# A relational graph-convolution kernel: the bias matmuls as a pair over two rows each, interleaved bn_stats, and work moved between the engines

## What is computed

```python
h = jnp.maximum(_layernorm(x, axis=-1), 0.0)          # eps 1e-5, no scale, no shift
x = x + relu( direction(h, W_fwd, Wg_fwd, b_fwd, bg_fwd, adj,   rels 2..40)
            + direction(h, W_bwd, Wg_bwd, b_bwd, bg_bwd, adj_t, rels 2..40)
            + direction(h, W_loop, Wg_loop, b_loop, bg_loop, adj_t, rel 1) )
# direction: hW = h @ W.T;  g = hW @ Wg.T
#   vals_r = (hW + b_r) * sigmoid(g + bg_r)
#   out[n] = sum over r and m of (adj[n, m] == r) * vals_r[m]
```

## Time and profile before

| | |
|---|---|
| runs | 123.61, 123.80, 123.98 us |
| median | 123.8 us |
| span of the profiled execution | 121.9 us (no separate time of this execution is shown) |
| busy in the span: PE, PE weight loads, DVE, ACT, POOL | 107.6, 102.9, 100.7, 103.8, 50.8 us |
| bytes moved | 25.41 MB, mean 208 GB/s |
| busy share of the DMA engines | nearly full until about 73 us, then under half |

### The profile page before, as it was taken

How to read it: one execution, slowest core, us unless ns; L and a number is a source line. 1 busy time by engine, 2 the same in 40 slices (tenths; PEclk the granted TensorE clock), 3 DMA queues, 4 the chain that set the end, 5 groups by cost and what they waited for, 6 DMA issues and landing times.

```text
span 121.9 us, 3211 instructions
## 1 busy us (share of the span) xinstructions
PE 107.6 (88%) x838; PEld 102.9 (84%) x838; DVE 100.7 (83%) x355; ACT 103.8 (85%) x230; POOL 50.8 (42%) x77
## 2 busy tenths in 40 slices
PE   0223999999999999999999999999999999999950
PEld 0012799999999999999999999999999999999940
DVE  3597878998998989898989898989899976666560
ACT  4039959999999999999999999999999999997400
POOL 6185344453627180908172635454363627220000
PEclk9999999999999999999999999999999999999996
DMA  2999999999999999999999980503132231405073
GB/s 57 312 291 255 296 290 292 291 290 295 288 297 280 320 282 278 314 338 323 321 341 317 327 235 16 152 21 114 58 93 79 64 110 33 139 7 170 19 229 104
DMA packets 50313, 25.41 MB, mean 208 GB/s; under 512 B 892, under 2 KB 50304, under 8 KB 50304
## 3 DMA queue, kind: packets, MB, share of 16 engines
q1 hardware_dynamic: 49952, 25.17, 75.4%
q10 hardware_dynamic: 288, 0.13, 0.4%
q0 software_dynamic: 64, 0.00, 0.0%
HBM read 16.91 MB, written 8.39 MB: 208 GB/s over the span
## 4 chain that ended last, share of the span: by engine, by line
PE 85%; DMA 4%; ACT 3%; DVE 2%; issue 1%; POOL 1%; POOLq 0%
PE psum L821 23%; PE psum L797 13%; PE psum L802 13%; PE psum L803 13%; PE psum L804 13%; PE psum L785 11%; DMA bias_in<-in_L_gnn_bg_loop 4%; ACT xn L433 2%; DVE x_all L609 1%; POOL bias_in L355 1%; PE psum L773 1%; DVE hT_lo L594 1%; ACT hT_hi L445 0%; ACT bias_hi L488 0%; ACT w_gT L492 0%
## 5 line engine op out<-in xcount | busy, mean ns | idle before, releaser
L433 ACT ACTIVATE xn<-x_all,shift,rstd 128x128 f32 (+1 forms) x128 | 55.4, 486 | 0.0
L371 POOL TENSOR_TENSOR rstd<-var_eps,minus_half 128x8 f32<-128x8 f32 (+1 forms) x17 | 26.6, 1563 | 50.2 <-DVE var_eps L569 50.2
L802 PE MATMUL psum<-w_hi,hT_hi 128*128 128x256 f32 x128 | 36.5, 285 | 0.0
L803 PE MATMUL psum<-w_lo,hT_hi 128*128 128x256 f32 x128 | 36.4, 284 | 0.0
L804 PE MATMUL psum<-w_hi,hT_lo 128*128 128x256 f32 x128 | 36.3, 283 | 0.0
L821 PE MATMUL psum<-vals,mask 128*128 128x128 f32 x256 | 33.5, 274 | 0.0
L584 DVE TENSOR_TENSOR vals<-psum,gate 128x512 f32<-128x512 f32 (+1 forms) x33 | 22.3, 675 | 11.3 <-ACT gate L457 11.3
L821 PEld LDWEIGHTS psum<-vals,mask 128*128 128x128 f32 x256 | 31.1, 191 | 0.0
L538 DVE BATCH_NORM_STATS2 stats<-x_all 128x6 f32 (+1 forms) x128 | 27.5, 278 | 2.3 <-DMA x_all<-in_x 2.1
L797 PE MATMUL psum<-bias_rows,ones_r 128*128 128x512 f32 x64 | 28.5, 445 | 0.2 <-DVE hT_lo L594 0.2
L803 PEld LDWEIGHTS psum<-w_lo,hT_hi 128*128 128x128 f32 x128 | 24.6, 192 | 2.9
(11 more groups left out here) (41 smaller groups left out, 36.7 us busy)
## 6 DMA issues: line engine op xcount, KB each, us to landing
adj_all<-in_adj SPq DMA_DIRECT2D x16, 512.0 KB, 6.6
x_all<-in_x SPq DMA_DIRECT2D x15, 512.0 KB, 5.8
out<-x_all SPq DMA_DIRECT2D x15, 512.0 KB, 3.3
x_all<-in_x SPq DMA_DIRECT2D x2, 256.0 KB, 3.7
out<-x_all SPq DMA_DIRECT2D x2, 256.0 KB, 2.4
w_raw<-in_L_gnn_W_loop ACTq DMA_DIRECT2D x1, 64.0 KB, 3.0
w_raw<-in_L_gnn_Wg_loop ACTq DMA_DIRECT2D x1, 64.0 KB, 3.8
bias_in<-in_L_gnn_b_loop POOLq DMA_DIRECT2D x1, 1.0 KB, 4.3
```

The costliest lines, as they stand in the source:

```text
L371: pool.tensor_tensor(rstd[:, p, cols], var_eps[:, p, cols], minus_half[:, cols], ALU.pow).then_inc(ready, 1)
L433: last = nc.scalar.activation(xn[:, s, j * D:j * D + D], x_all[:, bass.ds(g * GC + j * D, D)], ACT.Identity, bias=shift[:, p, k:k + 1], sc ...
L802: nc.tensor.matmul(to, hi, w_hi[:, :], start=False, stop=False)
L803: nc.tensor.matmul(to, hi, w_lo[:, :], start=False, stop=False)
```

## The change

The bias matmuls contract over two rows each. `ones_r`, `bias_in`, `bias_hi` and `bias_rows` have 64 partitions; the bias vectors are broadcast to all 64 by two loads from ACT's queue, issued after those of the weights. Rows 0 and 1 serve the first two graphs, rows 32 and 33 the other two, which lie in another group of 32 rows of the array. Both matmuls now stand ahead of all twelve products. The remainder is computed on all 64 partitions, and then four one-row copies put the high part on rows 0 and 32. `past` and `zeros` are gone.

bn_stats reads two graphs alternately, so that what it gives for the even elements is one graph's mean and variance and for the odd elements the other's. The seven small DVE instructions are gone, and POOL makes mean and variance with two instructions of its own ahead of the power. DVE normalises the fourth graph of each group, ACT the other three. The order of a step changes on ACT (relu, normalise, gate of t + 1, watch) and on DVE (messages, output, low_part, normalise, row_stats), without a special order for the start. POOL's steps are written out without a loop, coefficients ahead of the mask.

```diff
-            pool.dma_start(bias_in[:, 0, :], b_loop.to_broadcast([2, D])).then_inc(bias_loaded, 16)
-            pool.dma_start(bias_in[:, 1, :], bg_loop.to_broadcast([2, D])).then_inc(bias_loaded, 16)
...
+            def coefficients(p, lo, hi, var_done, at, done):
+
+                st = stats[:, p, lo // 2:hi // 2, :].rearrange("p k (e f) -> p k e f", e=2)
+                pool.tensor_scalar(var_eps[:, p, lo:hi].rearrange("p (k e) -> p k e", e=2), st[:, :, :, 2],
+                                   1.0 / D, EPS, ALU.mult, ALU.add).then_inc(var_done, 1)
+                pool.tensor_scalar(mean_neg[:, p, lo:hi].rearrange("p (k e) -> p k e", e=2), st[:, :, :, 1],
+                                   -1.0, 0.0, ALU.mult, ALU.add).then_inc(var_done, 1)
+                pool.wait_ge(var_done, 3 * at - 1)
+                pool.tensor_tensor(rstd[:, p, lo:hi], var_eps[:, p, lo:hi], minus_half[:, lo:hi], ALU.pow
+                                   ).then_inc(var_done, 1)
...
+            for t in range(-NORM, GROUPS):
+                if t == -NORM or (t % CHUNK == 0 and live(t + COEF)):
+                    c = (t + COEF) // CHUNK
+                    pool.wait_ge(stats_ready, c + 1)
+                    if c >= 2:
+                        pool.wait_ge(normed_dve, c * CHUNK - CHUNK)
+                        pool.wait_ge(normed_act, c * CHUNK - CHUNK)
+                    coefficients(c % 2, GROUP if c == 0 else 0, CG, var_ready, c + 1, coef_ready)
                 if live(t + MASK):
-                    edges(t + MASK, chunk_after(c, phase, MASK), (phase + MASK) % UNROLL)
...
+                    edges(t + MASK)
...
             def step(t, c, phase):
...
-                if live(t):
-                    sigmoid(t, phase)
-
-                if live(t + NORM):
-                    normalise(*norm, range(0, GROUP // 2))
                 if live(t + HT):
                     relu_turned(t + HT, (phase + HT) % UNROLL)
                 if live(t + NORM):
-                    normalise(*norm, range(GROUP // 2, GROUP))
+                    normalise(t + NORM, chunk_after(c, phase, NORM), (phase + NORM) % UNROLL)
+                if live(t + PROD):
+                    sigmoid(t + PROD, (phase + PROD) % UNROLL)
                 if (phase + 1) % CHUNK == 0 and live(t + 1):
                     watch(chunk_after(c, phase, 1), (phase + 1) % UNROLL)
 
+            act.dma_start(bias_in[:, 0:D], b_loop.to_broadcast([64, D])).then_inc(bias_loaded, 16)
+            act.dma_start(bias_in[:, D:2 * D], bg_loop.to_broadcast([64, D])).then_inc(bias_loaded, 16)
...
-                for j in range(GROUP):
+                if phase % CHUNK == 0 and late(g, 2 * CHUNK):
+                    dve.wait_ge(coef_ready, c - 1)
+                for j in range(0, GROUP, 2):
+                    k = (phase % CHUNK * GROUP + j) // 2
+                    last = nc.vector.bn_stats(
+                        stats[:, p, k, :],
+                        x_all[:, bass.ds(g * GC + j * D, 2 * D)].rearrange("p (b d) -> p d b", b=2))
...
+                for j in range(ON_ACT, GROUP):
                     k = phase % CHUNK * GROUP + j
...
+                    last = nc.vector.tensor_scalar(
+                        xn[:, s, j * D:j * D + D], x_all[:, bass.ds(g * GC + j * D, D)],
+                        mean_neg[:, p, k:k + 1], rstd[:, p, k:k + 1], ALU.add, ALU.mult)
+                last.then_inc(normed_dve, 1)
...
                 dve.wait_ge(bias_hi_ready, 1)
+                for n in range(2):
+                    nc.vector.tensor_tensor(bias_rows[:, n, :], bias_in[:, :], bias_hi[:, :].bitcast(FP32),
+                                            ALU.subtract).then_inc(bias_step, 1)
                 dve.wait_ge(bias_step, 2)
-                for n in range(2):
...
+                for at in (0, 32):
+                    for n in range(2):
+                        nc.vector.tensor_copy(bias_rows[at:at + 1, n, :], bias_hi[at:at + 1, :].bitcast(FP32)
+                                              ).then_inc(bias_step, 1)
...
+                if is_number(t, -3):
+                    split_weights()
+                    split_bias()
                 if live(t):
                     messages(t, phase)
-                if chunk_done:
-                    sums(*of)
                 if live(t - 1):
                     output(t - 1, (phase - 1) % UNROLL)
...
                 if live(t + HT):
                     low_part(t + HT, (phase + HT) % UNROLL)
...
+                if live(t + NORM):
+                    normalise(t + NORM, chunk_after(c, phase, NORM), (phase + NORM) % UNROLL)
+                if live(t + STATS):
+                    row_stats(t + STATS, chunk_after(c, phase, STATS), (phase + STATS) % UNROLL)
...
-                pe.wait_ge(normed, g + 1)
+                pe.wait_ge(normed_act, g + 1)
+                pe.wait_ge(normed_dve, g + 1)
...
-                for q in range(0, GROUP, 2):
-                    nc.tensor.matmul(prod_ps[s][:, q:q + 2, :, :], ones_r[:, :], bias_rows[:, :, :],
-                                     start=True, stop=False)
-                    for j in (q, q + 1):
-                        hi, lo = (h[:, s, j * N:j * N + N] for h in (hT_hi, hT_lo))
...
+                for n in range(2):
+                    nc.tensor.matmul(prod_ps[s][:, 2 * n:2 * n + 2, :, :], ones_r[32 * n:32 * n + 2, :],
+                                     bias_rows[32 * n:32 * n + 2, :, :], start=True, stop=False)
+                for j in range(GROUP):
+                    hi, lo = (h[:, s, j * N:j * N + N] for h in (hT_hi, hT_lo))
...
```

More of the change, by code:

```diff
@@ L245, in steps @@
                 step(t, t // CHUNK, t % UNROLL)
-        def filling(t):
-            return isinstance(t, int) and t < FILL_TO
         def is_number(g, n):
@@ L389, in edges @@
+            def edges(g):
+                if g % CHUNK == 0:
+                    arrived(pool, adj_loaded, g // CHUNK, g % UNROLL)
+                if g >= MASKS:
                     pool.wait_ge(summed, g - (MASKS - 1))
-                pool.tensor_copy(mask[:, phase % MASKS, :], adj_all[:, bass.ds(g * GC, GC)]
+                pool.tensor_copy(mask[:, g % MASKS, :], adj_all[:, g * GC:g * GC + GC]
                                  ).then_inc(mask_ready, 1)
-            def step(t, c, phase):
-                if live(t + MASK):
-                    edges(t + MASK, chunk_after(c, phase, MASK), (phase + MASK) % UNROLL)
-                if phase % CHUNK == 0 and live(t + COEF):
-                    coefficients(chunk_after(c, phase, COEF), (phase + COEF) // CHUNK % 2)
@@ L399, in _ @@
-            pool.wait_ge(first_stats, 1)
-            power(0, slice(0, GROUP), first_rstd, 1, first_coef)
-            steps(pool, step, -COEF, GROUPS)
+            pool.wait_ge(first_stats, 1)
+            coefficients(0, 0, GROUP, first_var, 1, first_coef)
+            for t in range(-NORM, GROUPS):
[6 more added lines that the diff above has]
+                    coefficients(c % 2, GROUP if c == 0 else 0, CG, var_ready, c + 1, coef_ready)
+                if live(t + MASK):
+                    edges(t + MASK)
@@ L418, in _ @@
             act.dma_start(w_raw[:, 1, :], Wg_loop).then_inc(w_loaded, 16)
-            def normalise(g, c, phase, graphs):
-                s, p = phase % 2, phase // CHUNK % 2
-                if graphs[0] == 0:
-                    if is_number(g, 0):
-                        act.wait_ge(first_coef, 1)
-                    elif phase % CHUNK == 0 or is_number(g, 1):
-                        act.wait_ge(coef_ready, c + 1)
-                    if late(g):
-                        act.wait_ge(turned, g - 1)
-                for j in graphs:
-                    k = phase % CHUNK * GROUP + j
-                    last = nc.scalar.activation(
-                        xn[:, s, j * D:j * D + D], x_all[:, bass.ds(g * GC + j * D, D)], ACT.Identity,
-                        bias=shift[:, p, k:k + 1], scale=rstd[:, p, k:k + 1])
-                if graphs[-1] == GROUP - 1:
-                    last.then_inc(normed, 1)
             def relu_turned(g, phase):
@@ L445, in relu_turned, with normalise @@
                 nc.scalar.activation(hT_hi[:, s, :], hT_ps[s], ACT.Relu).then_inc(hi_ready, 1)
+            def normalise(g, c, phase):
+                s, p = phase % 2, phase // CHUNK % 2
+                if is_number(g, 0):
+                    act.wait_ge(first_coef, 1)
+                elif phase % CHUNK == 0 or is_number(g, 1):
+                    act.wait_ge(coef_ready, c + 1)
+                if late(g):
+                    act.wait_ge(turned, g - 1)
+                for j in range(ON_ACT):
+                    k = phase % CHUNK * GROUP + j
+                    last = nc.scalar.activation(
+                        xn[:, s, j * D:j * D + D], x_all[:, bass.ds(g * GC + j * D, D)], ACT.Identity,
+                        bias=shift[:, p, k:k + 1], scale=rstd[:, p, k:k + 1])
+                last.then_inc(normed_act, 1)
```

(6 more changed lines are left out.)

156 lines of the change are left out of this document (36 added, 120 removed).

## The result

The changed kernel takes 132.80 us (median of 4 runs, 132.74 to 135.25) against 123.83 for the kernel before (4 runs): a ratio of 1.0724, 95% interval 1.0705 to 1.0744. It is 9.0 us slower; forecast were 127.8 us, 4.0 slower, with a range up to 131.5. Ratios and their intervals leave out executions over 1.5% above the fastest of the same kernel, medians and ranges take in all. The profiled execution is the one of 135.25 us (span 133.5), 2.4 us above the other three. In it TensorE's matmuls have the durations of its lower clock level until about 27 us, where in the kernel before they have them until 17; the other three executions have no trace. A later part comes back to this.

A forecast was written before the change was run, and what follows sets the result against it. PE was taken to bound the kernel at 3.21 us per group, ACT and DVE just keeping up. 123.8 + 3.0 for the bias matmuls' changes of shape + 1.0 for the fill = 127.8 us, range 117.0 to 131.5.

The forecast's parts named there:

- What bounds the kernel: Steady state: PE bounds at 3.21 us per group, ACT and DVE just keep up; 0.1 us per group gives 3.2 us.
- The bias matmuls: Steady state on PE: pair with both changes of shape costs 0.565 instead of 0.47 us per group, 3.0 us in all.
- the upper end of the bound: Bias matmuls on PE: emptying plus an uncovered load at both changes of shape, 0.795 us, a loss of 0.325 per group.
- The start: Fill: first products at 14.45 instead of 13.49 us, since ACT does relu of group 0 before normalising group 1: +1.0 us.
- the landing of the bias: Fill: bias loads behind the weights on ACT's queue land between 5.6 and 7.4 us, say 6.3.
- its end for the worst case: Fill: upper end of its cost, +2.5 us, by when the bias lands and what the one-row copies cost.
- Normalising on DVE: Steady state and fill: the fourth graph's normalising moves from ACT to DVE at 0.16 us each, with PE still the bound.
- (a): Bias matmuls on PE: pair runs side by side and the change of shape costs nothing, 117.3 us; chance 0.30.
- (b): DVE statistics: alternate reading halves bn_stats speed, 0.62 us each, and DVE takes PE's place, 123.7 us; chance 0.13.
- (c): Bias matmuls on PE: pair neither overlaps nor empties the array, 0.47 us as before, only the fill, 124.8 us; chance 0.09.
- its own bound: Steady state on PE: a group gains 0.235 us at the lower end and loses 0.325 at the upper, over 32 groups.
- The forecast's upper end: Whole kernel: 123.8 + 32 x 0.325 + 1.0 = 135.2 us, left out of the range.

The follow-up runs named there:

- one row group: Kernel before with both bias matmuls side by side ahead of the products, both over rows 0 and 1: 136.44 us, ratio 1.1001.
- two visits: Kernel before with each bias matmul over rows 0 and 1 where it stood, four changes of shape per group: 154.27 us, ratio 1.2275.
- the runs that have the small shape: Kernel before with two-row bias matmuls: in two row groups ahead of the products 129.39 us, separately in their old places 154.27, together over rows 0 and 1 136.44.
- everything but the pair: Changed kernel with bias matmuls over 128 rows, DVE normalising first, the fill in its old order and bias_hi behind the weight copies: 123.68 us, ratio 0.9995.

## Why the prediction was wrong

**What bounds the kernel: right.** PE bounded it before and after, and ACT and DVE kept up; a change of PE's time per group went to the end 31 times over (the forecast counted 32, which makes 0.1 us).

**The bias matmuls: what happens was right, its price too small.** The forecast said that each change of shape costs PE time, that the pair then runs side by side, and that both changes together cost more than the pair gains. All three came true: 3.38 us per group, 0.43 us from the pair's start to the first product (0.28 to 0.45 were said), PEld idle after the last transpose. It took 0.165 us per change, the part of a matmul's duration in which the next already runs, as the time in which the array empties. The runs show 0.19 to 0.20: 0.386 / 2 with one row group, 0.78 / 4 with two visits, (0.169 + 0.235) / 2 with the pair. The step that failed is that the load was put at nothing. On the return the first weights of the full shape lie open, 0.22 instead of 0.117 us to the next matmul; the upper end of the bound, 0.28, had such a load at each change and the chosen value at none. Of the 0.39 us for two changes this is 0.10, and the other 0.29 is 0.145 per change, somewhat under the 0.165. That the array is empty in that time is argued and not seen, since the ends of matmuls are modelled. Per group 0.169 instead of 0.095, so 5.2 instead of 3.0 us.

The Trainium skill, in "TensorEngine Tiling (Array Packing)", Key Properties, has a drain at such a change as a rule; the traces agree in that each change costs, 0.19 to 0.20 us. What "TensorE: Matmul & The Clock Gate" of the Trainium skill, Part 3, says of row groups that run at the same time agrees too: the two starts are 3 ns apart, and the pair takes 0.43 against 0.66 us in one row group.

**The start: the larger miss, +1.0 forecast, +3.6 measured.** The step that failed is the landing of the bias. It was set at 6.3 us, from 3.8 to 5.1 us between issue and landing for such loads; it was 8.86, since behind the weights in ACT's queue they took 6.1 and 6.5, and 5.3 to 6.7 in the other traces with that place. Everything after that point kept the distances of the forecast: first normalising 10.50 for 8.1, first transposes 13.15 for 10.45, second 16.07 for 13.35, first products 17.11 for 14.45, all late by 2.4 to 2.7 us, the 2.6 us of the landing. That the weight copies hang on the bias only by their order on ACT was read rightly, and its end for the worst case, +2.5, was still too low by 1.1. Of the 5.0 us between forecast and result 2.6 are this, 2.2 the changes of shape, and 0.2 are left.

**Normalising on DVE** was taken at 0.16 us and lasts 0.34 and more. It stayed hidden in the steady state. In the start the first transposes wait for it and begin 0.50 us after it (12.65 to 13.15), where 0.25 were set.

**The rivals.** (a), no price for the change of shape, fell in the changed kernel itself (3.38) and with the runs that have the small shape: 3.37, 3.98 and 3.60 us per group. Its one sign that came true, two starts within 0.01 us, is shared by the forecast. (b), bn_stats at half speed, fell with the trace of the changed kernel, where two are done in 0.76 us:

```profile
59.92 0.76 DVE L485 BATCH_NORM_STATS2 stats<-x_all 128x6 f32 x2
```

One lasts 0.42 us and the next starts 0.35 after it, as the forecast had it (0.35; the rival 0.62). "SBUF — State Buffer" of the Trainium skill, in its section on the DMA port swizzle, has a penalty for accesses that leave a 16-byte line; none shows in this instruction, whose second 128 elements cost 0.13 us or 1.0 ns each, as the 1.05 ns that the earlier trace rows give for the messages. (c), no overlap, fell with the one row group.

**The range.** The steady loss lay inside its own bound (5.2 of up to 10.4 us), the start outside (3.6 of up to 2.5): 123.8 + 5.2 + 2.5 is 131.5, the end of the range, and the 1.1 us beyond the start's bound carried the time over it. The forecast's upper end, 135.2, had been left out of the range. Its lower end is written as 117.0 where (a) comes to 117.3, which changes nothing.

## What to carry to other kernels

A matmul over two rows was not cheaper here than one over 128 rows filled up with zeros: alone between matmuls of the full shape it cost 0.39 us more. Two in different row groups save one matmul's columns only if what they save is above the two changes of shape around them: here 0.235 against 0.39 to 0.40 us. By these numbers, an estimate, small matmuls pay when what they save by running side by side between two changes is more than 0.4 us, or when nothing of the full shape stands beside them; no run here has either. In the fill, look for what hangs on a small load by order alone; moving one activation behind three others gave the kernel before 0.8 us. Work taken off engines that keep up with the bound brought nothing in the steady state, and the new order that came with it can cost at the start.

## What the runs showed of the hardware

- A change between matmuls over 128 rows and over two costs 0.19 to 0.20 us each way at the upper clock level, in a kernel that otherwise keeps a weight load under each matmul. Other numbers of rows weren't tried.
- Two 512-column matmuls in two row groups start 3 ns apart and take the time of one, to 0.01 us (0.43 for the pair, 0.42 for one alone).
- How long TensorE's durations stay at those of 1.2 GHz at the start varies in one kernel with the small shape: the last product at that level starts at 17.20 or at 21.09 us, and the total times lie in two clusters about 2.2 us apart. With two visits per group they stayed there until about 41 us. With 128 rows the last such product starts at 16.83 us in the kernel before and at 15.08 in the kernel with everything but the pair, whose 12 times form no such clusters. The column of the granted clock shows 1.00 for these stretches too; the durations tell them apart (0.41 and 0.28 us for a product). What decides between the two lengths stays open: no run tried it.
- DVE's normalising of a 128x128 tile lasts longer beside a running cast of POOL. Two rows of the changed kernel, the second inside POOL's:

```profile
62.54 0.34 DVE L504 TENSOR_SCALAR xn<-x_all,mean_neg,rstd 128x128 f32 x1
...
66.07 1.17 POOL L348 CAST mask<-adj_all 128x512 f32<-128x512 int32 x2
...
66.20 0.56 DVE L504 TENSOR_SCALAR xn<-x_all,mean_neg,rstd 128x128 f32 x1
```

In that trace all 19 that no cast overlaps last 0.34 or 0.35 us, and 12 of the 13 that stand beside one last 0.54 to 0.57. This was not tested by itself.
